# Choosing experts per batch beside the heads, and keeping split expert weights in memory

## The reference

```python
    x = x + _L0_xattn_ref(ctx_1024, _layernorm(x, axis=-1), ...)
    x = x + _L0_ffn_ref(_layernorm(x, axis=-1), ...)
    # in the experts:
    gate_scores = softmax(einsum('btd,de->bte', x, Wg) + bg)
    top1_mask = one_hot(argmax(gate_scores))
    top1_weight = sum(gate_scores * top1_mask)
    h = silu(einsum('btd,edh->bteh', x, W1) + b1)     # W1: 8 x 256 x 1024
    o = einsum('bteh,ehd->bted', h, W2) + b2          # W2: 8 x 1024 x 256
    y = sum(o * top1_mask) * top1_weight
```

## Time and profile before

| | |
|---|---|
| median of 3 runs | 2250.9 us (2250.64 to 2251.41) |
| the profiled execution | 2253.5 us, its span 2251.7 us |
| mean granted clock of TensorE | 0.967 |
| PE busy | 2051.4 us, 91% |
| DVE, ACT, POOL busy | 1623.1, 1500.4, 1379.9 us |
| read from HBM, written | 36.20 MB, 9.31 MB |

### The profile page before, as it was taken

The page is one execution under the profiler, slowest core; times in us unless marked ns, Lnnn a source line. Parts: engine busy times, 40 slices in busy tenths (PEclk is TensorE's granted clock), DMA queues, the critical chain, the costliest instruction groups (busy, mean ns, idle before and its releaser), DMA issues. The chain is left out here.

```text
span 2251.7 us, 63691 instructions
## 1 busy us (share of the span) xinstructions
PE 2051.4 (91%) x25812; PEld 1414.2 (63%) x25812; DVE 1623.1 (72%) x3037; ACT 1500.4 (67%) x1844; POOL 1379.9 (61%) x756
## 2 busy tenths in 40 slices
PE   2799999999999999999999999999999985589997
PEld 2266666667666666676666666766666654467775
DVE  7677777776788888767888877678888737664443
ACT  5277777774777777757777777477777763375554
POOL 3077777772777777727777777377777763254332
PEclk9699999999999999999999999999999997799999
DMA  4111111111111111111111111111111113251110
GB/s 161 32 32 43 33 38 33 33 43 48 40 38 32 33 33 43 34 53 35 35 33 33 43 33 43 44 38 33 33 40 36 38 44 108 69 180 36 37 37 23
DMA packets 90448, 104.24 MB, mean 46 GB/s; under 512 B 38177, under 2 KB 60373, under 8 KB 90037
## 3 DMA queue, kind: packets, MB, share of 16 engines
q1 hardware_dynamic: 86421, 90.85, 16.2%
q0 software_dynamic: 3744, 9.31, 1.3%
HBM read 36.20 MB, written 9.31 MB: 20 GB/s over the span
## 5 line engine op out<-in xcount | busy, mean ns | idle before, releaser
L502 POOL TENSOR_TENSOR probs_split<-probs,probs_split 128x1024 f16<-128x1024 f32 x576 | 1222.1, 2132 | 567.4 <-ACT probs_split L579 560.7
L572 ACT ACTIVATE probs<-score 128x1024 f32<-128x1024 f32 (+1 forms) x640 | 655.9, 1025 | 390.0 <-PE score L856 383.3
L714 DVE TENSOR_REDUCE max_parts<-aux 128x1 f32<-128x512 f32 x1024 | 682.9, 687 | 98.0 <-PE aux L856 90.3
L579 ACT ACTIVATE probs_split<-score 128x1024 f16<-128x1024 f32 (+1 forms) x640 | 653.1, 1020 | 0.0
L950 PE MATMUL acc<-values,probs_split 128*128 128x65 f16 x5120 | 553.7, 193 | 4.5 <-POOL probs_split L502 4.3
L954 PE MATMUL acc<-values,probs_split 128*128 128x64 f16 x4608 | 519.2, 194 | 0.0
L955 PE MATMUL acc<-values,probs_split 128*128 128x65 f16 x4608 | 516.9, 192 | 0.0
L950 PEld LDWEIGHTS acc<-values,probs_split 128*128 128x128 f16 x5120 | 463.3, 97 | 60.0 <-POOL probs_split L502 7.2
L856 PE MATMUL score<-q_both,k_high 128*128 128x512 f16 (+1 forms) x1280 | 485.9, 380 | 8.3 <-ACT probs_split L579 5.6
L856 PE MATMUL aux<-k_high,q_both 128*128 128x512 f16 (+1 forms) x1536 | 461.8, 335 | 30.5 <-DVE values L710 15.0
L856 PE MATMUL score<-q_max,k_low 65*128 65x512 f16 (+1 forms) x1280 | 488.8, 382 | 0.0
(11 more groups left out here) (166 smaller groups left out, 2425.3 us busy)
## 6 DMA issues: line engine op xcount, KB each, us to landing
k_high<-raw SPq DMA_DIRECT2D x128, 147.2 KB, 2.5
q_both<-raw SPq DMA_DIRECT2D x128, 128.0 KB, 2.4
zx_high<-in_L_ffn_W SPq DMA_DIRECT2D x16, 1024.0 KB, 5.5
k_low<-raw SPq DMA_DIRECT2D x64, 147.2 KB, 2.3
q_max<-raw SPq DMA_DIRECT2D x64, 128.0 KB, 2.3
att_rows<-in_x SPq DMA_DIRECT2D x4, 1024.0 KB, 8.1
x_res<-in_x SPq DMA_DIRECT2D x32, 128.0 KB, 2.2
x<-x_keep SPq DMA_DIRECT2D x32, 128.0 KB, 1.7
```

Source lines behind the costliest of these rows:

```text
L502: nc.gpsimd.tensor_tensor(out=low[0:r, :], in0=prob(h, j)[0:r, :], in1=high[0:r, :], op=ALU.subtract)\
L572: nc.scalar.activation(prob(h, j)[0:r, :], score[j % 2][0:r, :], ACT.Exp, scale=SCALE)\
L579: nc.scalar.activation(halves(h, j)[0][0:r, :], score[j % 2][0:r, :], ACT.Exp, scale=SCALE)\
L714: nc.vector.tensor_reduce(max_parts[g % 2][:, t, c:c + 1], bank[:, :], AX.X, ALU.max)\
```

## The change

1. **The choice is made per batch.** `Gate.choose` does for one batch (8 tiles) what the experts' stage did for all: largest logit, weight, first expert that has it, and running counts. It has nine parts. For batches 0 to 2 they are put on DVE after steps 0, 1, 2 and 4 to 9 of heads 28, 44 and 60 (`chosen_beside`, `CHOICE_STEPS`), with the exponential on ACT after step 2; for batch 3 they stand at the experts' start. The counts are kept by partition, so that only one column for each expert is left to be summed over partitions.
2. **One number per token.** The one-hot tables are float16 and carry the token's index alone. Weight, mean and inverse deviation are stored behind the row of x2 in memory (rows of 260 instead of 256 numbers) by one DMA of 1024 pieces of 16 bytes for each batch, and come with the gather.
3. **The experts' weights are split beside the heads.** Each of the 64 heads loads a quarter of a matrix (128x512), POOL rounds it after tile 2 and subtracts after tile 5, and SP stores both halves to `halves` in memory. The experts' stage loads the halves: expert 0 at its start, experts 1 to 7 when the first four gathers have landed. The splitting there, on ACT, POOL and DVE, is gone.
4. POOL takes the indices for gathers and scatters straight from the tables, without a copy into a column. The constants are made once, at the kernel's start.

```diff
+CHOICE_STEPS = [0, 1, 2, 4, 5, 6, 7, 8, 9]
+POWERS_STEP = 2
+PIECE_STEPS = (2, 5)
+def chosen_beside(h):
+    return h // H - 1 if h >= H and h % H == GATED_FROM + NT else None
...
+        def prefix(to, of, by):
+            vector.tensor_copy(to[:, 0:by, :], of[:, 0:by, :])
+            link(vector.tensor_tensor(out=to[:, by:NT, :], in0=of[:, by:NT, :], in1=of[:, 0:NT - by, :], op=ALU.add))
+        if part == 0:
+            link(vector.tensor_reduce(self.top[:, :], logits, AX.X, ALU.max))
+            vector.tensor_tensor(out=self.shifted[:, :, :], in0=logits, in1=per_token(self.top[:, :]), ...)
+        elif part == 1:
+            link(vector.tensor_tensor(out=self.marks[:, :, :], in0=logits, in1=per_token(self.top[:, :]), ...))
+            link(vector.tensor_tensor(out=self.marks[:, :, :], in0=self.marks[:, :, :], ...))
+        elif part == 2:
+            link(vector.tensor_reduce(self.first[:, :], self.marks[:, :, :], AX.X, ALU.min))
+            link(vector.tensor_tensor(out=chosen, in0=per_expert(self.e_less[:, :]), ...))
+        elif part == 3:
+            dve.wait_ge(self.powers_ready, b + 1)
+            link(vector.tensor_reduce(self.total[:, :], self.powers[:, :, :], AX.X, ALU.add))
+            vector.reciprocal(self.stat[:, ts, WEIGHT], self.total[:, :]).then_inc(self.weighed, 1)
+        elif part == 4:
+            prefix(self.reach[0], chosen, 1)
+        elif part == 5:
+            prefix(self.reach[1], self.reach[0], 2)
+        elif part == 6:
+            prefix(self.reach[0], self.reach[1], 4)
+        elif part == 7:
+            link(vector.tensor_tensor(out=after, in0=before, in1=self.reach[0][:, NT - 1, :], op=ALU.add))
+            link(vector.tensor_tensor(out=self.reach[1][:, :, :], in0=self.reach[0][:, :, :], in1=chosen, ...))
+        elif part == 8:
+            link(vector.tensor_tensor(out=self.reach[1][:, :, :], ..., in1=per_expert(before), op=ALU.add))
+            link(vector.tensor_tensor(out=self.marks[:, :, :], in0=self.reach[1][:, :, :], in1=chosen, op=ALU.mult))
+            link(vector.tensor_reduce(self.rank[:, ts], self.marks[:, :, :], AX.X, ALU.add))
...
             def head(h):
+                if h > 0:
+                    store_piece(h - 1)
+                load_piece(h)
+                if h > 0 and chosen_beside(h - 1) is not None:
+                    sp.wait_ge(gate.weighed, b + 1)
+                    sp.dma_start(stat_rows(x2_dram, b), gate.stat[:, b * NT:b * NT + NT, :])
...
                     low_half(h, j)
+                    if j == PIECE_STEPS[0]:
+                        pool.wait_ge(piece_loaded, 16 * (h + 1))
+                        at_least(pool, piece_stored, 2 * 16 * h)
+                        nc.gpsimd.tensor_copy(piece_out[0][:, :], piece_in[:, :])
+                    elif j == PIECE_STEPS[1]:
+                        nc.gpsimd.tensor_tensor(out=piece_out[1][:, :], in0=piece_in[:, :], in1=piece_out[0][:, :], ...)
...
+                    if j in CHOICE_STEPS and chosen_beside(h) is not None:
+                        gate.choose(dve, chosen_beside(h), CHOICE_STEPS.index(j))
                 take_rows(h)
...
+            load(0)
+            sp.wait_ge(gate.weighed, B)
+            sp.dma_start(stat_rows(x2_dram, B - 1), gate.stat[:, TT - NT:TT, :]).then_inc(gate.stat_stored, 16)
+            loaded(0)
+            for u in range(OWN):
+                sp.wait_ge(gathered[u], 16)
+            for e in range(1, E):
+                load(e)
...
+            pool.wait_ge(gate.stat_stored, 16 * B)
+            pool.wait_ge(read_ready, 1)
...
-                if EARLY + number(i, u) < WEIGHTS:
-                    low_weights(EARLY + number(i, u))
```

More of the change, by code:

```diff
@@ L2 @@
 from concourse import mybir
-from collections import namedtuple
 from contextlib import ExitStack
@@ L587, in head @@
                         high_half(of, jj)
+                    if j == POWERS_STEP and chosen_beside(h) is not None:
+                        gate.power(act, chosen_beside(h))
             def deviation(b, t):
@@ L994, in _, with experts @@
             whole_program(head, put_out)
-def experts(nc, x2_dram, gate, stage, e_loaded, W1, b1, W2, b2, out):
+def experts(nc, x2_dram, gate, split_dram, b1, b2, out):
     out_rows = out.rearrange("b n d -> (b n) d")
@@ L1161, in _ @@
-            for n in range(2, WEIGHTS):
-                load(n)
+            load(0)
[6 more added lines that the diff above has]
+                load(e)
+                if e > 1:
+                    loaded(e - 1)
+            loaded(E - 1)
         @block.gpsimd
@@ L1225, in _ @@
         def _(act):
[L1226 to L1239 removed]
+            gate.power(act, B - 1)
+            act.wait_ge(tile_ready, 1)
             def z_high_half(i, u):
@@ L1301, in _ @@
-            link(nc.vector.tensor_reduce(top[:, :], logits[:, :, :], AX.X, ALU.max))
-            nc.vector.tensor_tensor(out=work[0][:, :, :], in0=logits[:, :, :], in1=per_token(top[:, :]),
-                                    op=ALU.subtract).then_inc(shifted, 1)
-            tt(work[2][:, :, :], logits[:, :, :], per_token(top[:, :]), ALU.is_equal)
-            tt(work[2][:, :, :], work[2][:, :, :], per_expert(e_less[:, :]), ALU.mult)
-            link(nc.vector.tensor_reduce(first[:, :], work[2][:, :, :], AX.X, ALU.min))
@@ L1308, in _ @@
-            dve.wait_ge(powers, 1)
-            nc.vector.tensor_tensor(out=chosen[:, :, :], in0=per_expert(e_less[:, :]), in1=per_token(first[:, :]),
-                                    op=ALU.is_equal).then_inc(chosen_ready, 1)
-            link(nc.vector.tensor_reduce(place[:, :], work[1][:, :, :], AX.X, ALU.add))
-            link(nc.vector.reciprocal(rows[:, :, 1], place[:, :]))
-            nc.vector.tensor_copy(rows[:, :, 0], token[:, :])
-            nc.vector.tensor_copy(rows[:, :, 2], mean_var[:, :, 0])
@@ L1326, in _ @@
-            sums, spare = work[at], work[to]
-            link(nc.vector.tensor_scalar(counts[:, :], sums[:, TT - 1, :], float(P - 1), None, ALU.add))
+            for part in range(CHOICE_PARTS):
+                gate.choose(dve, B - 1, part)
+            nc.vector.tensor_copy(counted[:, :], gate.counts[:, B, :]).then_inc(counted_ready, 1)
+            dve.wait_ge(ranks, 1)
+            before, totals = turned[0][:, 0:E], turned[1][:, 0:E]
+            link(nc.vector.tensor_scalar(counts[:, :], totals, float(P - 1), None, ALU.add))
@@ L1341, in _ @@
-            tt(start[:, :], end[:, :], counts[:, :], ALU.subtract)
-            tt(spare[:, :, :], totals, sums[:, :, :], ALU.subtract)
-            tt(sums[:, :, :], before, spare[:, :, :], ALU.subtract)
-            tt(sums[:, :, :], sums[:, :, :], per_expert(start[:, :]), ALU.add)
-            tt(sums[:, :, :], sums[:, :, :], chosen[:, :, :], ALU.mult)
-            link(nc.vector.tensor_reduce(place[:, :], sums[:, :, :], AX.X, ALU.add))
-            link(nc.vector.tensor_copy(place_i[:, :], place[:, :]))
@@ new lines, in _ @@
+            link(nc.vector.tensor_reduce(start[:, :], before_e[:, :, :], AX.X, ALU.add))
+            nc.vector.tensor_tensor(out=end[:, :], in0=start[:, :], in1=counts[:, :], op=ALU.add)
+            link(nc.vector.tensor_tensor(out=start[:, :], in0=before, in1=start[:, :], op=ALU.add))
+            link(nc.vector.tensor_tensor(out=places[:, :, :], in0=gate.chosen[:, :, :],
+                                         in1=start[:, :].unsqueeze(1).to_broadcast([P, TT, E]), op=ALU.mult))
+            link(nc.vector.tensor_reduce(place[:, :], places[:, :, :], AX.X, ALU.add))
```

418 lines of the change are left out of this document (222 added, 196 removed).

## The result

The changed kernel took 2237.85 us (median of 5 runs, 2236.9 to 2241.37) beside 2251.41 for the kernel before on the same chip: a ratio of 0.9939, 95% interval 0.9925 to 0.9954. That is 0.6% faster, 13.6 us, where 2.6 were forecast. A second set (five runs of the changed kernel, nine of the one before) gave 0.9932 (0.9918 to 0.9946).

What follows compares the result with a forecast made beforehand. PE was taken to bound the attention, and a chain partly held up by POOL to bound the stretch between the stages. Gains of 37.1 less losses of 34.5 gave 2.6 us less, 2248 us, range 2222 to 2276.

Steps and rivals of the forecast that it cites:

- The gap: From last logits to first expert matmul: 58.9 us before, 25 forecast; the forecast is wrong if over 30.
- the three heads: Heads 28, 44 and 60: some 8 us longer than 25.1 each; forecast wrong if under 28 or over 38.
- The loss by the clock: In the attention: stalls of heads 28, 44 and 60 might bring TensorE's clock down, a loss not counted.
- chain between the stages: From last logits to first expert matmul: 34 us gained, bounds 29 and 38.
- experts' first tiles: First ten tiles of the experts' loop, now without splitting: 3.1 us gained, or nothing if loads slow the gathers.
- choice in three heads: `choose` on DVE in heads 28, 44 and 60: 8 us a head, 24 lost.
- normalising in gated heads: 24 gated heads: POOL's subtraction delays tiles and DVE's normalising, 0.3 each, 7 us lost, bounds 0 and 20.
- last two heads: Heads 62 and 63, POOL the bound: subtractions and roundings count in full, 3.5 us lost, bounds 2.3 and 4.6.
- The held time: DVE's `choose` instructions in heads 28, 44 and 60 wait for POOL: 12 x 0.73 = 8.8 us a head.
- rival 2: Heads 28, 44 and 60: DVE's chain falls into step with POOL, 17.4 us a head, 52 in all, 2276; chance 0.22.
- rival 1: Attention: held instructions cost nothing; choice costs 3 us, gated heads nothing, 2220 in all; chance 0.19.
- fourth case: Between the stages: gathers wait for the 1024 16-byte pieces, 3 to 7 us, 2251 to 2255; chance 0.07.

Runs made afterwards that it cites:

- experiment 5: Changed kernel with POOL's subtraction of a weight piece moved behind the head's last tile, after DVE's low half of it: 2242.94 us, ratio to the kernel before 0.9958.
- experiment 6: Changed kernel with weight pieces 0 and 1 made before the first head, so that heads 62 and 63 have none: 2237.02 us, one run.
- experiment 1: Changed kernel with the choice for batches 0 to 2 taken out of heads 28, 44 and 60 and made at the experts' start: 2232.67 us, one run.
- Experiment 7: Changed kernel with six subtractions of 128x2048 that serve nothing added on POOL at the experts' start: 2260.83 us, one run.
- experiment 2: Changed kernel with the choice spread, mostly one part to a head, behind DVE's low half of the last tile, where POOL idles: 2233.75 us, ratio to before 0.9912.
- experiment 8: Changed kernel with the choice for batches 0 to 2 moved to where output is made, after heads 31, 47 and 63: 2222.99 us, ratio 0.9871.
- experiment 3: Changed kernel with the choice spread over heads, each part behind step 1, where POOL works: 2261.04 us, 1.0039 of the kernel before.
- experiment 4: Changed kernel with the choice spread into POOL's pauses, its 19 instructions in heads 28, 44 and 60 each replaced by a useless reduction: 2241.51 us.

## Why the prediction was right, and where it was off

The range (2222 to 2276) and the forecast's own range (2237 to 2262) hold 2237.85, the latter at its edge; the forecast of 2248 was 10 too high. The gap was to be under 30 and is 25.0; the three heads were to last 28 to 38 and last some 31 (25.1 and 6.2). The loss by the clock that the prediction named and did not count came in head 44 alone and was small: its two sides lost 0.4 to 0.7 more than those of heads 28 and 60, held time included (6.4 to 6.6 against 5.9). The mechanism stood in the large terms; the losses were set too large. The 2.6 that were forecast were the small difference of 37.1 and 34.5, and the sign of the change hung on the choice. In us, plus is gained:

| step | forecast | measured | from |
|---|---|---|---|
| chain between the stages | +34 | +33.9 | 58.9, then 25.0 |
| experts' first tiles | +3.1 | +5.2 | ten tiles 76.0, then 72.1; and first matmul to third transpose 11.45, then 10.10, but 11.45 and 11.57 in experiments 5 and 6 |
| choice in three heads | -24 | -18.6 | experiment 1 |
| normalising in gated heads | -7 | -4.1 | 0.33 and 0.02 by turns, experiment 5 |
| last two heads | -3.5 | -3.0 | experiment 6: 2.2 up to L975 of head 63, 0.8 from there to the last logits |
| not forecast | | +1.3, +1.5, +0.4 | ahead of head 0; between batches (184.3, then 182.8); last tiles |

These come to 16.6, against spans that differ by 16.7. The last row and 1.3 of the second can be chance: the places vary by as much between kernels that do the same there.

**The chain.** The total is right, 25.0, but two errors of 1.5 cancelled in it. Up to the indices (1932.09) it took 17.8 where the sum had 19.3: change of stage 0.3 (forecast 1), choice 4.1 (4.3), PE's count 0.5 (1.0), tables 7.5 (7.8). From the indices to the first matmul it is 7.25, not 5.8, and was 6.9. The second gather was to start one issue behind the indices, and started 2.36 behind them, against 2.19 with the column copies: the first one starts 0.91 after the indices, where it was 0.55 with its copy. So taking the indices straight from the tables gained nothing there; why the first gather starts so late no run shows. Experiment 7 shows by addition that six instructions of POOL are worth 24 us, which is most of the 33.9.

**The choice** is the term that was mis-sized most, and rightly understood only in half. Own time was 3.9 (the parts of experiment 2) to 4.1 (between the stages), forecast 4.2 to 4.3. The held time was set at 12 x 0.73 = 8.8, as if each instruction met POOL at random. The groups of the changed kernel (four batches, the last unheld) show otherwise:

```profile
L284 DVE TENSOR_TENSOR shifted<-logits,top 128x64 f32<-128x64 f32 x4 | 6.6, 1662 | 0.1
L279 DVE COPY reach<-reach 128x16 f32<-128x16 f32 (+1 forms) x8 | 5.9, 733 | 0.2
L279 DVE CAST reach<-chosen 128x8 f32<-128x8 f16 x4 | 4.0, 988 | 0.0
L293 DVE TENSOR_TENSOR chosen<-e_less,first 128x64 f16<-128x64 f32 x4 | 3.5, 883 | 0.1
L289 DVE TENSOR_TENSOR marks<-marks,e_less 128x64 f32<-128x64 f32 x4 | 0.9, 225 | 0.1
```

Of a part's instructions at most one is held here; a second that follows a held one slips through before POOL's next (L289 0.22). The excess over the same instructions unheld in experiment 8 is 20.2 us, 6.7 a head. So rival 2, in which the second always meets POOL, fell here, and rival 1, in which the choice costs 3 us in all, too (18.6). What rival 2 describes does occur where POOL's instructions stand without a pause, as in head 63 of experiment 3, where this second instruction follows one of 1.10:

```profile
1872.19 2.11 DVE L317 TENSOR_TENSOR reach<-reach,chosen 128x64 f32<-128x64 f32 x1
```

Subtracting 5.5 us of spare time came near, since 4.1 + 6.7 less 6.2 leaves 4.6, but the rule behind it was wrong. Spare time is not a sum that any instruction of the head may draw on. Experiments 2 and 3 put the same instructions at one place of each head and lost their whole length, held or not; experiment 4 put as much over nine places and lost 0.9 to 1.7. By these runs an instruction costs its length at its place, held time included, less the idle time behind it up to DVE's next work that PE waits for. For single parts up to 2.1 us long this held; behind the two longest (3.15 and 2.38 us) TensorE's granted clock fell to 0.50 for 3.4 us, and the 1.7 that this can cost make up the rest. For the nine places of the changed kernel's choice the rule was not worked out place by place.

**The gated heads.** L953 was forecast at 1.8 and measured 1.69; a bare 0.3 was taken for each head and it is 0.33 in every second one, 0.02 in the others. The rule of the place fits within 0.1: the normalising is 0.77 longer, and in the kernel before DVE idled 0.67 behind it where values of 128x384 follow, the heads that lose 0.02, but 0.34 where values of 128x256 follow, the heads that lose 0.33.

**The last two heads, the pieces, the gathers.** Subtraction 1.16 and rounding 0.61, as forecast. The 16-byte pieces took 4.8 us to land (median of the four batches; 7.7 for the last, issued at 1918.21) and nobody waited for them: the gathers' indices came at 1932.09. So the read-modify-write below 512 bytes of which the Trainium skill speaks ("DMA: Bandwidth & Descriptors", Specifications) changed no time here; whether it happened, or doubled the time as the prediction's fourth case took it, no run shows.

## What to carry to other kernels

Before adding work to an engine with spare time, read where in the repeating stretch that time lies: an instruction costs its length at its place less the idle time right behind it, and an average over the stretch says little. Where two engines hold each other up, a cost depends on phase, repeats from round to round while nothing is moved (29.04, 29.03 and 29.03 for the near sides of heads 28, 44 and 60), and changes when anything else is moved; move such work to a stretch in which the other engine is still, as `put_out` was for POOL here, rather than to a small pause. Judge several such moves together as well as one by one: the subtraction's move lost 5 us with the choice in its old place and gained with the choice gone. Where a measured stall costs more than its length, look at TensorE's granted clock right behind it.

## What was not expected of the hardware

- The spread choice in experiment 3: three instructions of 0.22 us in one head cost 3.8 us, up to 1.7 of them as TensorE's granted clock fell to half behind the stall, and the whole is slower than the kernel before the change.
- A copy of eight numbers was held 1.55 us by a memset on POOL, which reads nothing, while two-input instructions beside the first memset were not (experiment 7; the one behind the copy took 1.52).
- One-hot tables in float16 took 1.46 and 1.15 us, nearly as long as those in float32 (1.46 and 1.22); both have an operand that is broadcast.
